# A transformer mixer on one core: ScalarE issues a store and a load, the first router layer and `x` of layer 1 in other banks, `product` 0 and the norm's `scale` moved

## The chip, the cores and the metric

One core of a Trainium2 chip runs the kernel. The metric is the device time of one execution in microseconds; below half a per cent or so nothing is claimed.

## The reference

Input `x` is 8 x 1024 tokens of 256 numbers. The output is the input plus two branches of its layer norm:

```python
xn = _layernorm(x)
x = x + attn(xn) + ffn(xn)
# attn: 16 heads of 16; heads 0-3 causal over all 1024 keys, heads 4-15 causal over the last 64;
#       softmax, times V, times w_out, plus biases
# ffn, with Q = xn @ W_Q.T, K = xn @ W_K.T and a second pair Q @ W_inv.T, K @ W_inv.T:
xV = einsum('btd,kdr->btkr', Q_side, V)            # 8 experts of 64
cum_yW = cumsum(einsum('btd,kdr->btkr', K_side, W), axis=1)
h = gelu(Q_side @ router_w1.T + router_b1)         # router, exact gelu
weights = softmax(h @ router_w2.T + router_b2 + expert_bias)
out = einsum('btkr,kdr->btd', xV * cum_yW * weights[..., None], U) + weights @ b
out = out / n_valid
# ffn = (fwd + alpha * inv) @ W_O.T
```

## The kernel before, in words

The weights of all layers are folded once at the start: `W_O` into `U`, `W_Q` into the router and `V`. Every float32 product that needs full precision is made of three of fp32r parts (high x high, high x low, low x high; helper `mms`, L684). Then 16 chunks of 512 tokens pass (two per sequence). A chunk with an even number is the first half of a sequence and has few blocks of global attention (6 tiles of 128 keys x 256 queries), one with an odd number has 14.

The order of work is written out by hand. `Plan.add` lists stages (`x`, `c`, `weigh`, `product`, `gscore`, ...), `weave` mixes a main list with a side list, and each of the five engine programs walks the one list and issues its own part of each stage. So the place of a stage in the list sets its place in the in-order queue of every engine, SyncE with its DMA issues among them. `uses` names the PSUM bank (0 to 7) that a stage takes; the n-th user waits until the one before it is read out.

One chunk `ch` passes these phases, while the next one is prepared:

- **experts and peaks.** For each of 8 expert layers j: `x` (6 matmuls, bank 2, copied by ScalarE to `prod[j % 3]`, L1039), `weigh` (GpSimd multiplies it by the spread router weights in `wide[j % 3]`, L1517), `c` (6 matmuls, bank 3), `product` (VectorE multiplies bank 3 into `prod`, L1323; ScalarE makes the high part PH, L1049; GpSimd the low part PL, L1522), `mix` (TensorE sums onto the output in banks 0 and 1, L795). `c` of layer j+1 can't begin before `product` j has read bank 3. Between them stand the peaks: TensorE computes all scores once (L817 local, L831 global, banks 4 to 7) over masks that ScalarE lays down (L1055), and VectorE takes the largest of each row (L1240, L1247).
- **local attention**, with the next chunk's `turn`, `parts` (queries and keys in three bf16 parts; VectorE L1211 reads the bank), and `hidden` (first router layer, 4 x 6 matmuls, banks 2, 3, 4, 3).
- **global attention**: `gscore` (L890), exponentials (L1075), `gav` (L908), and in their midst `logits`, `gates`, `gate_parts` (router softmax on VectorE, L1279 to L1316), `values`, and the norm of chunk `ch + 2` in nine steps (`NORM`; the last, `scale`, is L1174).
- **handover**: `weigh` 0, `x` 1, `weigh` 1, `cturn` and `chigh` of the context's second half (L1351, L1081), `x` 2, `weigh` 2, `crest` (L1356), then the next chunk's first group, which was `product` 0.

The router weights travel through DRAM: `gate_parts` stores `weights_t` in four DMAs of 8 rows to `weights_d` (L1648) and the bf16 rows to `rows_d` (L1654); `wide` loads each row spread over 64 partitions (L1678), two DMAs per layer; `weight_rows` loads `WT` (L1663) for `open`, the bias matmul (L761). All DMAs are issued by SyncE. Ahead of the store stand the `stacks` of the next chunk (eight DMAs, `area<-parts_d`, L1605), behind it `Vs` (L1618) and the global stacks (L1607).

## Time and profile before

| | |
|---|---|
| median of 3 runs | 1487.54 us (1483.8 to 1489.47) |
| the profiled execution | 1489.6 us, span 1487.9 us |
| granted clock, mean | 0.983 |
| busy: TensorE, VectorE, ScalarE, GpSimd | 92%, 68%, 52%, 39% |
| DMA: bytes, share of the 16 engines by SyncE's queue | 150.59 MB, 39.1% |

The profile is of one execution. TensorE is the busiest engine; the share of the others is an average over phases of different kinds, and has to be read phase by phase. A wait in the views is the idle time of an engine just before an instruction, with what ended it.

### The profile page before, as it was taken

The numbers are of one execution on the slowest core, as the hardware profiler recorded it, in microseconds if no ns is written. First come the engines' busy times: TensorE is split into PE (matmuls) and PEld (weight loads), VectorE is DVE, ScalarE is ACT, GpSimd is POOL, SyncE is SP. The second block draws the span as 40 slices with busy tenths as digits, with TensorE's granted clock in tenths as the row PEclk, the third lists the DMA queues.
The fourth block names the chain that finished last, engine by engine and source line by source line (L and its number), as shares of the span: only waits on it lengthen the run. The fifth ranks groups of instructions, "written<-read, shape, count | busy, mean of one in ns | idle before, by whom it ended". The sixth has DMA issues, their size and how long they took to land.

```text
span 1487.9 us, 35980 instructions
## 1 busy us (share of the span) xinstructions
PE 1368.7 (92%) x14481; PEld 1034.5 (70%) x14481; DVE 1004.9 (68%) x2082; ACT 775.5 (52%) x1368; POOL 580.1 (39%) x663
## 2 busy tenths in 40 slices
PE   5978999999999989998999999999999989999986
PEld 4567685777848677586867768577775868667673
DVE  6667777567755867567775667567885577756661
ACT  2434537464564635645375554646356453755544
POOL 1024343443424344253434524244452434345350
PEclk9999999999999999999999999999999999999997
DMA  8430625326162541616344171623517153441610
GB/s 186 106 94 25 164 70 130 116 67 160 44 158 67 124 123 48 168 33 152 95 117 113 40 187 39 155 90 100 148 38 175 35 147 100 112 117 41 175 37 15
DMA packets 166614, 152.88 MB, mean 103 GB/s; under 512 B 37809, under 2 KB 149808, under 8 KB 166448
## 3 DMA queue, kind: packets, MB, share of 16 engines
q1 hardware_dynamic: 166448, 150.59, 39.1%
q8 instruction: 114, 1.87, 0.5%
q14 instruction: 52, 0.43, 0.1%
HBM read 108.57 MB, written 35.65 MB: 97 GB/s over the span
## 4 chain that ended last, share of the span: by engine, by line
PE 64%; DVE 13%; ACT 7%; issue 7%; DMA 5%; POOL 1%; SPq 1%; ACTq 0%; POOLq 0%; DVEq 0%
PE PS L684 32%; PE PS L795 10%; PE PS L831 4%; DMA weights_d<-weights_t 3%; ACT HE L1075 3%; PE PS L890 3%; PE PS L919 3%; PE PS L817 2%; DVE prod L1211 2%; PE PS L973 2%; PE PS L908 2%; DMA rest<-weights_d 2%; ACT HE L1067 2%; DVE area L1214 1%; PE PS L876 1%
## 5 line engine op out<-in xcount | busy, mean ns | idle before, releaser
L684 PE MATMUL PS<-XH,WH 128*128 128x512 f32 x512 | 219.8, 429 | 29.1 <-DVE prod L1211 14.5
L1522 POOL TENSOR_TENSOR PL<-prod,PH 128x512 fp32r<-128x512 f32 x128 | 164.9, 1289 | 207.9 <-ACT PH L1049 207.9
L1049 ACT ACTIVATE PH<-prod 128x512 fp32r<-128x512 f32 x128 | 80.8, 632 | 272.9 <-DVE prod L1323 257.0
L1517 POOL TENSOR_TENSOR prod<-prod,rest 128x512 f32<-128x512 f32 x96 | 123.1, 1284 | 244.2 <-DMA rest<-weights_d 167.8
L1247 DVE TENSOR_REDUCE block_peak<-PS 128x4 f32<-128x512 f32 x288 | 179.8, 684 | 49.0 <-PE PS L831 48.9
L684 PE MATMUL PS<-XH,WL 128*128 128x512 f32 x512 | 203.7, 398 | 0.0
L684 PE MATMUL PS<-XL,WH 128*128 128x512 f32 x512 | 203.5, 398 | 0.0
L1075 ACT ACTIVATE HE<-PS 128x512 f32<-128x512 f32 (+1 forms) x320 | 159.9, 552 | 34.4 <-PE PS L890 31.6
L1500 POOL TENSOR_SCALAR_AFFINE_SELECT HE<-HE 128x256 f32<-128x256 f32 x128 | 51.5, 408 | 305.5 <-ACT HE L1075 302.0
L1323 DVE TENSOR_TENSOR prod<-PS,prod 128x512 f32<-128x512 f32 x128 | 87.8, 686 | 100.2 <-PE PS L684 79.0
L684 PEld LDWEIGHTS PS<-XH,WH 128*128 128x128 f32 x512 | 96.9, 189 | 70.4 <-DVE prod L1211 21.1
L1039 ACT ACTIVATE prod<-PS 128x512 f32<-128x512 f32 x128 | 75.7, 591 | 114.5 <-PE PS L684 104.2
L795 PE MATMUL PS<-UH,PH 128*128 128x256 f32 x512 | 133.1, 293 | 0.0
L684 PE MATMUL PS<-CH,WH 128*128 128x512 f32 x256 | 109.6, 428 | 24.7 <-DVE prod L1323 24.7
L1240 DVE TENSOR_REDUCE peak<-PS 128x4 f32<-128x512 f32 x192 | 119.0, 682 | 19.1 <-PE PS L817 19.1
L795 PE MATMUL PS<-UL,PH 128*128 128x256 f32 x512 | 127.5, 282 | 0.0
L1339 DVE STREAM_TRANSPOSE craw<-PS 128x512 f32<-128x512 f32 x64 | 45.5, 712 | 102.3 <-PE PS L908 96.4
L684 PEld LDWEIGHTS PS<-XH,WL 128*128 128x128 f32 x512 | 96.8, 189 | 22.5
L890 PE MATMUL PS<-area 99*128 99x256 bf16 (+1 forms) x640 | 101.4, 267 | 10.5 <-ACT HE L1075 7.3
L684 PEld LDWEIGHTS PS<-XL,WH 128*128 128x128 f32 x512 | 97.8, 191 | 14.2
L1067 ACT ACTIVATE HE<-PS 128x512 f32<-128x512 f32 x192 | 105.2, 594 | 2.4 <-PE PS L851 2.4
L684 PE MATMUL PS<-CH,WL 128*128 128x512 f32 x256 | 103.8, 406 | 0.0
(190 smaller groups left out, 3047.9 us busy)
## 6 DMA issues: line engine op xcount, KB each, us to landing
parts_d<-area SPq DMA_DIRECT2D x32, 768.0 KB, 5.0
area<-parts_d SPq DMA_DIRECT2D x128, 192.0 KB, 7.9
rest<-weights_d SPq DMA_DIRECT2D x192, 128.0 KB, 3.0
area<-parts_d SPq DMA_DIRECT2D x32, 576.0 KB, 7.9
tok<-in_L_attn_x_dram SPq DMA_DIRECT2D x16, 512.0 KB, 6.3
xt<-in_L_attn_x_dram SPq DMA_DIRECT2D x16, 512.0 KB, 4.2
wide<-weights_d SPq DMA_DIRECT2D x64, 128.0 KB, 3.1
out_dram<-xt SPq DMA_DIRECT2D x16, 512.0 KB, 3.8
```

What stands on the lines that cost most here:

```text
L684: ins = e.matmul(ps, a, b, start=first and k == 0, stop=last and k == n - 1, skip_group_check=True)
L795: ins = e.matmul(out_half(t), (PH, PL)[part][:, h, t * P:(t + 1) * P], u[:, j, :], start=False, stop=False, skip_group_check=True)
L890: ins = e.matmul(psum(i, lo=HALF * a + lo, hi=HALF * (a + 1)), KG[0:KSTK, g, j * P:(j + 1) * P], QS[0:KSTK, g, half * HALF + lo:(half + 1) ...
L1039: e.activation(prod[:, j % 3, :], psum(2), ACT.Copy).then_inc(bank_read[2])
L1049: e.activation(PH[:, h, :], prod[:, j % 3, :], ACT.Copy).then_inc(phi)
L1067: e.activation(HE[:, k, :], psum(i), ACT.Exp, scale=SCALE).then_inc(bank_read[i])
L1075: e.activation(two(HE[:, k, :], lo), two(psum(i), lo), ACT.Exp, scale=SCALE).then_inc(bank_read[i])
L1240: e.tensor_reduce(peak[:, t, 4 * grp:4 * (grp + 1)], psum(i).rearrange("p (a k) -> p a k", a=4), AX_X, ALU.max).then_inc(bank_read[i])
L1247: e.tensor_reduce(block_peak[ch % NC][:, t, :, j], psum(i).rearrange("p (a k) -> p a k", a=4), AX_X, ALU.max).then_inc(bank_read[i])
L1323: e.tensor_tensor(prod[:, r, :], psum(3), prod[:, r, :], ALU.mult).then_inc(bank_read[3])
L1517: e.tensor_tensor(prod[:, j % 3, :], prod[:, j % 3, :], wide[j % WIDE], ALU.mult).then_inc(weighed)
L1522: e.tensor_tensor(PL[:, j % 2, :], prod[:, j % 3, :], PH[:, j % 2, :].bitcast(F32), ALU.subtract).then_inc(plo)
```

## The change

- `weights_d` becomes a copy of `weights_t` (128 x 256) and is stored in one DMA, for all chunks. `wide` reads each row in two halves of 256.
- In odd chunks (`by_scalar`) ScalarE issues this store (after `values` 0) and the first `wide` load (after the last but two of the global groups). In even chunks SyncE still does.
- For all chunks SyncE's bf16 store (`weight_parts`) comes behind the first `wide` loads instead of ahead of them.
- `hidden` uses banks 4, 2, 3, 4. `x` of layer 1 uses bank 7 from chunk 1 on.
- `product` 0 is added behind `chigh` and ahead of `x` 2.
- `scale` of the norm moves from the global phase of one chunk to behind the first group of peaks in the next, from chunk 2 on.

```diff
@@ -114,6 +114,10 @@
+    def x_bank(ch, j):
+        return 7 if ch and j == 1 else 2
@@ -191,14 +195,14 @@
     def add_hidden(ch, j):
-        add_on("hidden", ch, j, uses=[f"bank{(2, 3, 4, 3)[j]}", exp_use()])
+        add_on("hidden", ch, j, uses=[f"bank{(4, 2, 3, 4)[j]}", exp_use()])
...
     def add_x(ch, j, part):
-        add("x", ch, j, part, uses=["bank2"] if part == 0 else [])
+        add("x", ch, j, part, uses=[f"bank{x_bank(ch, j)}"] if part == 0 else [])
@@ -267,7 +271,8 @@
             order.append([(add_c, ch, j, part) for part in range(2)] if j else [])
-            order[-1].append((add_product, ch, j))
+            if j or not ch:
+                order[-1].append((add_product, ch, j))
             if j:
@@ -296,9 +301,14 @@
         add("gate_parts", ch)
-        for j in range(WIDE):
+        for j in range(1 if by_scalar(ch) else 0, WIDE):
             add_wide(ch, j)
+        add("weight_parts", ch)
         add("weight_rows", ch)
+    def by_scalar(ch):
+        return ch % NC == 1
@@ -309,8 +319,9 @@
         at_ = len(order) // 3
-        for n in range(len(NORM)):
-            order[at_ + n * (len(order) - at_) // len(NORM)].append((add, "norm", ch, n))
+        steps = len(NORM) - (1 if ch > 1 else 0)
+        for n in range(steps):
+            order[at_ + n * (len(order) - at_) // steps].append((add, "norm", ch, n))
@@ -397,6 +408,8 @@
         run(experts[0] + peaks[0])
+        if ch and nxt:
+            add("norm", ch + 1, len(NORM) - 1)
         weave(experts[1:split], peaks[1:])
@@ -433,6 +446,9 @@
             side += [[(add_values, ch + 1, 0)], [(add_values, ch + 1, 1)]]
+            if by_scalar(ch + 1):
+                side[-2].append((add, "weights_store", ch + 1))
+                order[-3].append((add_wide, ch + 1, 0))
             side[0].append((add, "crest", ch, 0))
@@ -447,6 +463,7 @@
         if nxt:
+            add_product(ch + 1, 0)
             run([(add_x, ch + 1, 2, part) for part in range(2)])
@@ -537,7 +554,7 @@
         peak_d = [nc.dram_tensor(f"peak_d_{n}", (3 * k, C), BF16, kind="Internal").ap() for n, k in (("local", NL), ("global", NG))]
-        weights_d = nc.dram_tensor("weights_d", (2 * KE, C), F32, kind="Internal").ap()
+        weights_d = nc.dram_tensor("weights_d", (P, HALF), F32, kind="Internal").ap()
         rows_d = nc.dram_tensor("rows_d", (3, 2 * KE, C), BF16, kind="Internal").ap()
@@ -673,6 +690,29 @@
+        def store_weights(e, q, ch):
+            q.wait_ge(weights_turned, ch + 1)
+            for i in range(WIDE):
+                q.wait_ge(wide_in[i], 16 * 2 * (use(f"wide{i}", "wide", ch, i) - 1))
+            e.dma_start(weights_d, weights_t[:, :]).then_inc(weights_out, 16)
+        def load_weights(e, q, ch, j):
+            q.wait_ge(weights_out, 16 * (ch + 1))
+            if j >= WIDE:
+                q.wait_ge(weighed, nth("weigh", ch, j - WIDE))
+            elif j == 2:
+                q.wait_ge(weighed, nth("weigh", ch - 1, 5))
+            else:
+                q.wait_ge(part3, nth("parts", ch, 0, DB - 1))
+                q.wait_ge(clo, DB * (ch + 1))
+                if ch == 0:
+                    q.wait_ge(bias_in, 16 * 15)
+            by_half = weights_d[2 * 32 * (j // KB):2 * 32 * (j // KB + 1), :].rearrange("(h e) t -> e h t", h=2)
+            for k in range(2):
+                n = 2 * (j % KB) + k
+                e.dma_start(wide[j % WIDE][R * k:R * (k + 1), :].rearrange("p (h t) -> p h t", h=2), by_half[n:n + 1].to_broadcast([R, 2, HALF])).then_inc(wide_in[j % WIDE], 16)
@@ -738,7 +778,7 @@
                     ch, = key
-                    q.wait_ge(bank_read[3], use("bank3", "hidden", ch, 3))
+                    q.wait_ge(*out_of_bank("hidden", ch, 3))
                     take(7, *stage)
@@ -763,10 +803,11 @@
                     ch, j, part = key
+                    i = x_bank(ch, j)
                     if part == 0:
-                        take(2, *stage)
+                        take(i, *stage)
                     n = 3 * part
-                    ins = mms(psum(2), weight_pairs(COL_X + j * P, XH, XL)[n:n + 3], first=part == 0, last=part == 1)
+                    ins = mms(psum(i), weight_pairs(COL_X + j * P, XH, XL)[n:n + 3], first=part == 0, last=part == 1)
                     if part == 1:
@@ -1024,6 +1065,14 @@
+                elif kind == "weights_store":
+                    store_weights(e, q, *key)
+                elif kind == "wide":
+                    ch, j = key
+                    if j == 0 and by_scalar(ch):
+                        load_weights(e, q, ch, j)
                 elif kind == "x":
@@ -1036,7 +1085,8 @@
                                 q.wait_ge(part3, nth("parts", ch, 0, j // 2))
-                        e.activation(prod[:, j % 3, :], psum(2), ACT.Copy).then_inc(bank_read[2])
+                        i = x_bank(ch, j)
+                        e.activation(prod[:, j % 3, :], psum(i), ACT.Copy).then_inc(bank_read[i])
@@ -1306,7 +1356,7 @@
                     q.wait_step()
-                    q.wait_ge(weights_out, 16 * 4 * ch)
+                    q.wait_ge(weights_out, 16 * ch)
                     q.wait_ge(rows_cast, ch)
@@ -1512,7 +1562,8 @@
                     ch, j = key
-                    q.wait_ge(bank_read[2], use("bank2", "x", ch, j, 0))
+                    i = x_bank(ch, j)
+                    q.wait_ge(bank_read[i], use(f"bank{i}", "x", ch, j, 0))
                     q.wait_ge(wide_in[j % WIDE], 16 * 2 * use(f"wide{j % WIDE}", "wide", ch, j))
@@ -1639,13 +1690,11 @@
                     ch, = key
-                    q.wait_ge(weights_turned, ch + 1)
-                    for i in range(WIDE):
-                        q.wait_ge(wide_in[i], 16 * 2 * (use(f"wide{i}", "wide", ch, i) - 1))
-                    for w in range(2):
-                        for h in range(2):
-                            row = 32 * (2 * w + h)
-                            e.dma_start(weights_d[KE * w:KE * (w + 1), h * HALF:(h + 1) * HALF], weights_t[row:row + KE, :]).then_inc(weights_out, 16)
+                    if not by_scalar(ch):
+                        store_weights(e, q, ch)
+                elif kind == "weight_parts":
+                    ch, = key
                     q.wait_ge(rows_cast, ch + 1)
@@ -1664,18 +1713,8 @@
                     ch, j = key
-                    q.wait_ge(weights_out, 16 * 4 * (ch + 1))
-                    if j >= WIDE:
-                        q.wait_ge(weighed, nth("weigh", ch, j - WIDE))
-                    elif j == 2:
-                        q.wait_ge(weighed, nth("weigh", ch - 1, 5))
-                    else:
-                        q.wait_ge(part3, nth("parts", ch, 0, DB - 1))
-                        q.wait_ge(clo, DB * (ch + 1))
-                        if ch == 0:
-                            q.wait_ge(bias_in, 16 * 15)
-                    for k in range(2):
-                        e.dma_start(wide[j % WIDE][R * k:R * (k + 1), :], weights_d[2 * j + k:2 * j + k + 1, :].to_broadcast([R, C])).then_inc(wide_in[j % WIDE], 16)
+                    if j or not by_scalar(ch):
+                        load_weights(e, q, ch, j)
```

How the rows move at the handover from chunk 2 to chunk 3, which stands for all eight into an odd chunk. Line numbers differ between the two kernels.

ScalarE, from the last exponentials to `product` 0, before:

```order
L1075 ACTIVATE HE<-PS 128x512 [waits he5_read,gscores_ps]
L1075 ACTIVATE HE<-PS 128x512 [waits he0_read,gscores_ps]
L1008 ACTIVATE Va<-PS 128x32x16 [waits values_ps]
L1075 ACTIVATE HE<-PS 128x2x128 [waits he1_read,gscores_ps]
L1075 ACTIVATE HE<-PS 128x2x128 [waits he2_read,gscores_ps]
L1039 ACTIVATE prod<-PS 128x512 [waits plo,x_ps]
L1081 ACTIVATE PH<-craw 128x512 [waits split1_read,ctx_turned]
L1039 ACTIVATE prod<-PS 128x512 [waits part3,x_ps]
L1049 ACTIVATE PH<-prod 128x512 [waits split0_read,bank3_read_out]
```

and with the change:

```order
L1049 ACTIVATE Va<-PS 128x32x16 [waits values_ps,vs_in]
L697 DMA weights_d<-weights_t 128x256 [waits wide1_in,wide2_in,wide0_in,weights_turned]
L1125 ACTIVATE HE<-PS 128x512 [waits he5_read,gscores_ps]
L1125 ACTIVATE HE<-PS 128x512 [waits he0_read,gscores_ps]
L1049 ACTIVATE Va<-PS 128x32x16 [waits values_ps]
L1125 ACTIVATE HE<-PS 128x2x128 [waits he1_read,gscores_ps]
L1125 ACTIVATE HE<-PS 128x2x128 [waits he2_read,gscores_ps]
L714 DMA rest<-weights_d 64x2x256 [waits clo,part3,weights_out]
L714 DMA rest<-weights_d 64x2x256
L1089 ACTIVATE prod<-PS 128x512 [waits plo,x_ps]
L1131 ACTIVATE PH<-craw 128x512 [waits split1_read,ctx_turned]
L1099 ACTIVATE PH<-prod 128x512 [waits split0_read,bank3_read_out]
```

The two kinds of DMA are new on this engine, the load waits for the store's landing (`weights_out`), and PH (L1099, before L1049) stands ahead of the copy of `x` 2.

SyncE, from the weights' store to the rows' loads, before:

```order
L1648 DMA weights_d<-weights_t 8x256 [waits wide1_in,wide2_in,wide0_in,weights_turned]
L1648 DMA weights_d<-weights_t 8x256 x3
L1654 DMA rows_d<-weights_b 3x8x256 [waits rows_in,rows_cast]
L1654 DMA rows_d<-weights_b 3x8x256 x3
L1678 DMA rest<-weights_d 64x512 [waits clo,weights_out]
L1678 DMA rest<-weights_d 64x512 x3
L1678 DMA wide<-weights_d 64x512 [waits weighed]
L1678 DMA wide<-weights_d 64x512
L1663 DMA WT<-rows_d 48x1x512 [waits opened,rows_out]
L1663 DMA WT<-rows_d 32x1x512
```

and with the change:

```order
L714 DMA rest<-weights_d 64x2x256 [waits clo,weights_out]
L714 DMA rest<-weights_d 64x2x256
L714 DMA wide<-weights_d 64x2x256 [waits weighed]
L714 DMA wide<-weights_d 64x2x256
L1703 DMA rows_d<-weights_b 3x8x256 [waits rows_in,rows_cast]
L1703 DMA rows_d<-weights_b 3x8x256 x3
L1712 DMA WT<-rows_d 48x1x512 [waits opened,rows_out]
L1712 DMA WT<-rows_d 32x1x512
```

The store and one pair of loads are gone, and the four issues to `rows_d` stand behind the loads.

VectorE, from the context's last transposition to the second peaks, before:

```order
L1343 TENSOR_TENSOR ctok<-craw,cinv 128x16x16 [waits dve_step]
L1174 TENSOR_SCALAR tok<-tok,mv,var 128x256 [waits dve_step]
L1174 TENSOR_SCALAR tok<-tok,mv,var 128x256 x3
L1351 STREAM_TRANSPOSE craw<-ctok 128x512
L1356 TENSOR_TENSOR PL<-craw,PH 128x512 [waits ctx_hi]
L1323 TENSOR_TENSOR prod<-PS,prod 128x512 [waits c_ps,weighed]
L1240 TENSOR_REDUCE peak<-PS 128x4 [waits lpeaks_ps] x4
L1323 TENSOR_TENSOR prod<-PS,prod 128x512 [waits c_ps,weighed]
L1367 TENSOR_TENSOR xt<-PS,xt 128x512 [waits out_ps,residual_in]
L1367 TENSOR_TENSOR xt<-PS,xt 128x512 [waits split1_read]
```

and with the change:

```order
L1393 TENSOR_TENSOR ctok<-craw,cinv 128x16x16 [waits dve_step]
L1219 TENSOR_SCALAR var<-var 128x4 [waits dve_step]
L1221 TENSOR_TENSOR var<-var 128x4 [waits dve_step]
L1401 STREAM_TRANSPOSE craw<-ctok 128x512 [waits dve_step]
L1373 TENSOR_TENSOR prod<-PS,prod 128x512 [waits c_ps,weighed]
L1406 TENSOR_TENSOR PL<-craw,PH 128x512 [waits ctx_hi]
L1290 TENSOR_REDUCE peak<-PS 128x4 [waits lpeaks_ps] x4
L1224 TENSOR_SCALAR tok<-tok,mv,var 128x256 x4
L1373 TENSOR_TENSOR prod<-PS,prod 128x512 [waits c_ps,weighed]
L1417 TENSOR_TENSOR xt<-PS,xt 128x512 [waits out_ps,residual_in]
L1417 TENSOR_TENSOR xt<-PS,xt 128x512 [waits split1_read]
```

`scale` (L1174, now L1224) has gone from ahead of `cturn` to behind four peak reductions, `product` (L1323, now L1373) ahead of `crest` (L1356, now L1406).

## Rows read from the trace of the kernel before

**Rows 1.** The page, busy time of each engine.

```profile
PE 1368.7 (92%) x14481; PEld 1034.5 (70%) x14481; DVE 1004.9 (68%) x2082; ACT 775.5 (52%) x1368; POOL 580.1 (39%) x663
```

**Rows 2.** TensorE's waits, whole span: for whom, us in total, times, longest.

```profile
PE PS L684 <- DVE prod L1323: 24.7, 11, 3.7
PE PS L684 <- DVE prod L1211: 14.5, 15, 1.0
...
PE PS L684 <- ACT prod L1039: 10.3, 15, 0.7
```

**Rows 3.** The same view, from 160 to 1487 us.

```profile
PE PS L684 <- DVE prod L1323: 17.5, 8, 3.7
```

**Rows 4.** Three of eight stretches at odd handovers: busy times, PEclk, DMA, GB/s.

```profile
339.00:361.00 22.00, 19.28 (x176) 14.91 (x174) 16.45 (x46) 10.88 (x20) 7.95 (x9) 0.92 0.65 159
513.00:535.00 22.00, 17.64 (x164) 13.40 (x164) 15.20 (x45) 8.30 (x16) 7.18 (x9) 0.84 0.63 150
...
1036.00:1058.00 22.00, 19.24 (x203) 13.89 (x202) 17.98 (x57) 11.26 (x22) 8.32 (x11) 1.00 0.76 170
```

**Rows 5.** The chain that ended last, 340 to 352.2: start, us, what.

```profile
340.08 6.16 DMA weights_d<-weights_t
...
346.82 3.06 DMA rest<-weights_d
350.01 1.27 POOL prod L1517
351.31 0.70 DVE prod L1323
352.06 0.51 PE PS L684
```

**Rows 6.** Timeline of TensorE: first and third group of local peaks.

```profile
348.94 1.08 PE L817 MATMUL PS<-area 96*64 96x128 bf16 x32
...
361.09 1.08 PE L817 MATMUL PS<-area 96*64 96x128 bf16 x32
```

**Rows 7.** Stretches; the last three columns are PEclk, DMA share, GB/s.

```profile
340.00:345.00 5.00, 5.00 (x53) 3.76 (x52) 4.32 (x23) 1.64 (x4) 1.55 (x4) 1.00 1.02 197
...
366.00:371.00 5.00, 5.00 (x42) 4.27 (x40) 4.56 (x9) 2.44 (x4) 3.06 (x3) 1.00 0.22 59
```

**Rows 8.** Timeline of SyncE's DMA issues: start, us of all issues, line, what.

```profile
339.07 1.30 SPq L1648 DMA_DIRECT2D weights_d<-weights_t  x4
340.47 3.03 SPq L1654 DMA_DIRECT2D rows_d<-weights_b  x4
346.25 2.44 SPq L1678 DMA_DIRECT2D rest<-weights_d  x4
...
350.07 1.93 SPq L1663 DMA_DIRECT2D WT<-rows_d  x3
...
353.56 5.22 SPq L1607 DMA_DIRECT2D area<-parts_d  x8
...
365.68 3.41 SPq L1635 DMA_DIRECT2D peak_d_local<-peak_t_local  x4
370.35 0.28 SPq L1638 DMA_DIRECT2D area<-peak_d_local  x1
```

**Rows 9.** Timeline of ScalarE, 338 to 361.

```profile
341.86 0.66 ACT L1075 ACTIVATE HE<-PS 128x256 f32<-128x256 f32 x2 [0.18 <-PE PS L890]
345.82 0.60 ACT L1039 ACTIVATE prod<-PS 128x512 f32<-128x512 f32 x1 [3.30 <-PE PS L684]
...
358.02 2.40 ACT L1055 ACTIVATE PS<-peak_mask_l 128x512 f32<-128x512 bf16 x4 [0.63 <-DVE peak L1240]
```

**Rows 10.** Timeline of VectorE, 346 to 356.

```profile
346.12 1.38 DVE L1174 TENSOR_SCALAR tok<-tok,mv,var 128x256 f32<-128x256 f32 x4
...
351.92 2.48 DVE L1240 TENSOR_REDUCE peak<-PS 128x4 f32<-128x512 f32 x4
...
355.49 0.69 DVE L1367 TENSOR_TENSOR xt<-PS,xt 128x512 f32<-128x512 f32 x1 [0.50 <-PE PS L919]
```

## The prediction

> **What bounds the kernel now.** I read the page first. TensorE is busy for 92% of the span [rows 1], so anything that delays it delays the end, and anything hidden under it is free. The view of TensorE's waits then tells which delays the change can touch. Three kinds stand there [rows 2]: a multiplication waits for VectorE's `product` (L1323) 24.7 us in 11 cases, the first router layer for VectorE's query part (L1211) 14.5 us in 15, `x` for ScalarE's copy out of bank 2 (L1039) 10.3 us in 15. After 160 us the first kind is 17.5 us in 8 cases, the longest 3.7 [rows 3]: once per handover into an odd chunk (0 to 1, 2 to 3, ... 14 to 15). The other 7.2 us lie before 160 us, in the start-up, and I leave them alone. The 15 of the other two kinds are one per handover, about 0.97 and 0.69 us each.
>
> The stretches around the 8 odd handovers show what such a wait costs beyond itself [rows 4]: the granted clock of TensorE, 1.00 elsewhere, is 0.92 over 22 us in five of them, 0.84 in the one with the 3.7 us wait, 1.00 in two. That is 5 x 1.76 + 3.5 = 12.3 us of lost matmul time: after the idle stretch TensorE runs for a while at 1.2 instead of 2.4 GHz.
>
> The chain of waits at the handover 2 to 3 says who is late [rows 5]: the weights' store to DRAM lands 6.16 us after its last issue, the spread load takes 3.06, the weighing on GpSimd 1.27, `product` on VectorE 0.70, and only then `c` of layer 1 starts at 352.06. TensorE was ready at 350.02, when its peak matmuls (L817, 348.94 + 1.08) were done [rows 6]. Why does a 32 KB store take 6.16 us? The 16 DMA engines are busy all the time from 340 to 345 (1.02), with the stacks of the next chunk, which SyncE issued just before on the same queue; from 366 to 371 the share is 0.22 [rows 7], and there the small peak store is waited out 1.26 us after its issues (365.68 + 3.41 to 370.35) [rows 8]. So the store stands in line behind the stacks.
>
> **The change part by part**, at that handover.
>
> 1. Banks of the first layer. Hidden 1 no longer takes the bank that L1211 has yet to read; it takes bank 2, free earlier, and hidden 2, which takes bank 3, comes 1.4 us later. Bank 4 was used in this place before. The wait of 0.97 goes: 15 x 0.97 = **-14.5**. `x` of layer 1 in bank 7 takes away the wait of `x` of layer 2 for the copy: 15 x 0.69 = **-10.3**. ScalarE and GpSimd do the same work, and nothing else in rows 2 waits there.
>
> 2. Store by ScalarE. The store is one DMA of 128 x 256 (128 KB) for four of 8 KB. The weights turn 1 us earlier (term 1), at 338.1; in ScalarE's order the issue stands behind a copy, and I take 338.4, against SyncE's last of four, which ended at 339.07 + 1.30 = 340.4 [rows 8]. No row shows a DMA issued by ScalarE. Its landing is bounded below by the 1.26 us of the peak store plus 128 KB at the 197 GB/s of [rows 7] (0.65) and an issue, some 2.5 us, above by the 6.16 us of the store in line, a little more for its size. I take 3.6, nearer the short end, because its queue holds nothing else: it lands at 342.0. By the Trainium skill (DMA: Bandwidth & Descriptors, Queues, rings and completion order) SP and ACT each own one row of rings and every DMA engine goes round between the rows packet by packet, which would let it overtake; the same page (Issuing engines are not separate DMA queues) says that issuing from several engines only saves the sequencer's time. No run here shows either; the second is a rival below.
>
> 3. First spread load by ScalarE. It waits for the landing behind the last exponentials, which end at 342.5 before [rows 9], 341.8 now. Two issues of 0.6, landing 3.06 after the second begins (pieces of 1 KB for 2 KB: 0 to 0.6 more), 1.27 and 0.70 [rows 5]: 342.0 + 0.6 + 3.1 + 2.0 = 347.7. TensorE is ready at 350.0 - 1.7 = 348.3. The wait goes with 0.6 us to spare: **-17.5**, and the clock with it: **-12.3**.
>
> 4. `scale` of the norm (1.38 us on VectorE) leaves the path before `cturn`, and moves behind the first four peak reductions; `product` 0 now goes ahead of the rest of the context. With `product` done at 347.7 VectorE goes on: rest of the context 348.4, four reductions of 0.62 to 350.9, `scale` 352.3, `product` 1 353.0, two additions of 0.69 354.4, four reductions 356.9 [rows 10]. Each reduction lets ScalarE write a mask of 0.60 [rows 9]: the last is ready at 357.5. TensorE's third group of peaks came 361.09 - 352.06 = 9.0 us after `c` [rows 6], of which 1.7 were the slow clock; it would begin at 348.3 + 7.3 = 355.6 and end a microsecond later, and now ends at 357.8. Cost 1.2, taken as 1.5: 8 x 1.5 = **+12**. At the even handovers TensorE comes only 1.7 us earlier, and I take nothing.
>
> 5. ScalarE's issues. The store's takes 0.3 to 0.65 us (SyncE's of 8 rows and of 128) out of a stretch in which TensorE waits for exponentials: 8 x 0.6 = **+4.8**. What else queues behind the two issues of the load is the copy of `x` 1, which before had waited 3.30 us for TensorE [rows 9]: no cost, if the store has landed. For the load and SyncE's neighbouring loads colliding I add 8 x 0.5 = **+4**.
>
> 6. SyncE's order. Now loads 1 and 2 (four issues, 2.44 us), the bf16 rows' store (3.03), its landing (1.26 as the peak store), then the rows' loads (1.93), `Vs` (1.56 up to 353.56) and the global stacks (5.22) [rows 8]. Before, the last issue ended at 358.8; now 342.0 + 15.4 = 357.4, 1.4 us earlier, while TensorE is 4 us earlier. The last stack is in some 3.1 us after its issue begins, at 360.0. Its first reader, two pieces of 1.5 us behind the third group of peaks, comes at 361. No cost, but a microsecond of cover; if it is gone, the global peaks are late next. At the even handovers, where the same order puts the rows behind three loads, TensorE's phase is longer and I take nothing.
>
> Sum: -14.5 - 10.3 - 17.5 - 12.3 + 12 + 4.8 + 4 = **-33.8**. The profiled execution took 1489.6 us (span 1487.9), 2 us above the median 1487.5 of the runs shown; the same difference from the median gives **1454**.
>
> **The rivals.** (A, forecast) as above, 0.60.
>
> (B) The store overtakes, but the gain runs into VectorE and SyncE. VectorE is busy for 16.45 of 22 us there [rows 4]; if the third group waits 3 us and not 1.5, and the rows or global stacks come a microsecond late, 8 x 2.5 = 20 us go back: 1474, or 1470 if one holds in part. For it: the margins of 1 us in terms 3 and 6. Against it: these waits would have to lie wrong by a microsecond in all eight, and a wait that only moves along the path is counted once. 0.20, at 1471.
>
> (C) The store doesn't overtake: it waits for the stacks and lands at 346.0. Then ScalarE stands still from 341.8, `product` ends at 351.7 and `c` starts 0.35 us earlier than before, but with a wait of 3.4 us in place of 2.0. The handover at 513 had such a wait, and its clock was 0.84 for 0.92: 1.7 us more. 8 x (1.7 - 0.35) = +10.8 against 15 waits for the copies of which the 7 even handovers keep 1.66 each, -11.6: about no change, 1487. This is what the skill's second sentence would give. 0.12.
>
> (D, slower) ScalarE becomes the gate. Its queue is in order, and in odd chunks the first mask is in bank 7, which waits for the copy of `x` 1, which waits behind the load, which waits for the store. If the store lands at 347.6, 1.6 us later than in C, each odd handover is 2.95 us longer: +23.6 - 11.6 = +12, 1499. It passes the half per cent from a landing at 347.1, some 8.5 us after the issue. For it: four times the bytes, twice the pieces in the loads, two queues at once on full DMA engines. Against it: 6.16 us is what the whole line took. 0.08.
>
> **How the numbers follow.** A measurement of this kernel can tell about 0.5% (7.4 us) from no change. A and B are faster, C is within, D slower; a few cases of C fall on either side: faster 0.81, same 0.11, slower 0.08. The range goes down to 1442, where terms 4 to 6 cost half of what I put, and up to 1482, past B and to the edge of C.
>
> **What would show it.** Right: no wait for L1373 (the new line of `product`) after 160 us, none for the query part, none for the copy of `x`; a granted clock of 1.00 at the handovers; the store landing within 4 us of its issue while the stacks still move; new small waits of TensorE at the peaks (L817's successor) of 1 to 1.5 us. Wrong: `weights_d` still in the chain with 6 us, ScalarE idle until it lands, TensorE waiting for a mask or for `product` over 3 us at odd handovers; or the waits gone and the time the same, which would mean that the peaks or the global stacks took their place.

## The result, and the profile after

The changed kernel takes 1492.36 us (median of 18 runs, 1487.78 to 1497.88), the kernel before on the same chip 1486.33 (18 runs). The ratio is 1.004, 95% interval 1.0029 to 1.0051: 6.0 us slower (4.3 to 7.6), which is the near edge of what a measurement can tell from no change. Forecast were 1454 and a range of 1442 to 1482; the result lies outside it. The profiled execution took 1492.45 us, its span is 1490.7; the spans of the two profiled executions (1490.7 and 1487.9) are 2.8 us apart, less than half of what the medians are. Of the executions of the later runs, two passed at a low clock throughout (2119.69 us at 0.559, 1638.86 us at 0.75), and the medians given leave them out.

The page of the changed kernel, busy times and DMA queues:

```profile
PE 1371.8 (92%) x14481; PEld 1042.8 (70%) x14481; DVE 1006.3 (68%) x2082; ACT 773.5 (52%) x1368; POOL 582.6 (39%) x663
...
q1 hardware_dynamic: 180656, 149.01, 39.8%
q10 hardware_dynamic: 3456, 3.15, 0.8%
```

Queue q10 is new: it is ScalarE's. TensorE is 3.1 us longer busy than in [rows 1] with the same instructions, and its mean granted clock is 0.975 for 0.983, so more of the time passed at 1.2 GHz. How much of the 3.1 us is the clock's isn't settled: busy time does not follow the clock alone (one of the runs below has 0.975 with 1366.5 us).

TensorE's waits in the whole span (for whom, us in total, times, longest), which answer to [rows 2]:

```profile
PE PS L724 <- DVE prod L1373: 27.1, 11, 3.6
PE PS L844 <- ACT prod L1089: 18.3, 8, 3.2
...
PE PS L801 <- DMA WT<-rows_d: 3.8, 1, 3.8
```

The waits of 14.5 and 10.3 us are gone, all 30 of them, as forecast. But `product` (L1373) is waited for 2.4 us more, and there are two new waits: in 8 handovers 18.3 us for ScalarE's copy out of bank 7 (L1089, ahead of the first mask), and once, at 97.6 us in chunk 0, 3.8 us for the bf16 rows (0.2 before). The sum of these waits was 24.7 + 14.5 + 10.3 + 0.2 = 49.7 us and is 27.1 + 18.3 + 3.8 = 49.2; that with the 3.1 us of longer busy time makes +2.6, and the spans differ by 2.8. The waits have moved, not gone.

The chain of waits at the handover 2 to 3 (start, us, what), which answers to [rows 5]:

```profile
339.01 8.65 DMA weights_d<-weights_t
347.68 0.63 ACTq L714
348.33 4.86 DMA rest<-weights_d
353.33 1.27 POOL prod L1568
354.63 0.70 DVE prod L1373
355.37 2.93 PE PS L724 x6
```

`c` of layer 1 starts at 355.37, 3.3 us later than before. The store is issued a microsecond earlier than the last of four in [rows 8], and lands 8.65 us after that, at 347.66, instead of at 346.24. The load takes 4.86 for 3.06.

The landing is better counted from the stacks. SyncE's issue of the eight local stacks, in the kernel before:

```profile
330.12 5.38 SPq L1605 DMA_DIRECT2D area<-parts_d  x8
```

and in the changed kernel, with the load that waits for the store:

```profile
331.26 5.39 SPq L1656 DMA_DIRECT2D area<-parts_d  x8
347.67 1.26 SPq L714 DMA_DIRECT2D rest<-weights_d  x2
```

So 1.1 of the 3.3 us were there already when the stacks were issued. From the start of that issue to the weights' landing it is 16.1 us before and 16.4 with the change, though the last issue of the store comes 10.0 us after that start before and 7.75 us now. The weights came 2.2 us earlier against the stacks and landed no earlier.

ScalarE stands still meanwhile. Its timeline, with the idle time before an instruction in brackets, against [rows 9]:

```profile
339.01 0.33 ACTq L697 DMA_DIRECT2D weights_d<-weights_t  x1
...
341.78 0.66 ACT L1125 ACTIVATE HE<-PS 128x256 f32<-128x256 f32 x2 [0.18 <-PE PS L931]
347.68 1.53 ACTq L714 DMA_DIRECT2D rest<-weights_d  x2
349.31 0.60 ACT L1089 ACTIVATE prod<-PS 128x512 f32<-128x512 f32 x1 [6.88 <-issue]
```

The last exponentials end at 342.44; then nothing until the store has landed. The copy of `x` 1, which before waited for TensorE, comes at 349.31, and TensorE, which needs its bank for the first mask, waits for it.

Why the store needs 8.65 us shows in the DMA queues (packets, MB, share). First the stretch 341 to 343, two microseconds after the store's issue, then 345 to 347:

```profile
q1 hardware_dynamic: 450, 0.45, 111.3%
```

```profile
q1 hardware_dynamic: 175, 0.16, 38.7%
q10 hardware_dynamic: 144, 0.13, 24.9%
```

From 339 to 345 no packet of q10 is moved; the first packet of q10 is moved in 345 to 345.5, six microseconds after its issue, when the stacks are nearly through. The store is 144 packets. By the Trainium skill (DMA: Bandwidth & Descriptors, Queues, rings and completion order) every DMA engine goes round between the rings packet by packet; with that, packets of q10 should stand beside those of q1 from 339 or 340 on, and the trace does not agree. The other sentence of the same page in the Trainium skill that the prediction drew on (Issuing engines are not separate DMA queues), that issuing from several engines saves only the sequencer's time, fits what is seen.

The granted clock at the same stretches as [rows 4] (last columns PEclk, DMA share, GB/s):

```profile
339.00:361.00 22.00, 16.63 (x126) 12.78 (x126) 13.32 (x40) 7.23 (x15) 6.74 (x8) 0.77 0.66 142
513.00:535.00 22.00, 17.75 (x172) 13.04 (x171) 13.65 (x45) 8.07 (x16) 6.77 (x8) 0.92 0.72 146
...
1036.00:1058.00 22.00, 15.96 (x139) 12.06 (x138) 13.21 (x44) 8.33 (x16) 6.76 (x8) 0.92 0.71 146
```

Over the seven such stretches from 339 on the clock is three times 0.77 or 0.78 and four times 0.92; before it was four times 0.92, once 0.84 and twice 1.00. With two waits of about 3 us in each, where there was one of about 2, more of the stretch passes at 1.2 GHz.

### The profile page after: what moved, and what is told of

Read it like the earlier page. It is cut to its first block, busy times and chain, and to the rows that moved or that the text cites. A ratio compares the mean times of both kernels' runs of the same rounds, so it can differ in the third digit from the quotient of the medians.

```text
span 1490.7 us, 35948 instructions
## 1 busy us (share of the span) xinstructions
PE 1371.8 (92%) x14481; PEld 1042.8 (70%) x14481; DVE 1006.3 (68%) x2082; ACT 773.5 (52%) x1368; POOL 582.6 (39%) x663
## 4 chain that ended last, share of the span: by engine, by line
PE 68%; DMA 8%; DVE 7%; ACT 7%; issue 5%; POOL 3%; SPq 0%; ACTq 0%; POOLq 0%; DVEq 0%
PE PS L724 35%; PE PS L836 10%; DMA weights_d<-weights_t 5%; PE PS L872 4%; ACT HE L1125 3%; PE PS L931 3%; PE PS L960 3%; DMA rest<-weights_d 3%; PE PS L917 3%; PE PS L858 2%; ACT HE L1117 2%; PE PS L1014 2%; PE PS L949 2%; PE PS L892 2%; DVE prod L1373 1%
## 5 line engine op out<-in xcount | busy, mean ns | idle before, releaser
L1573 POOL TENSOR_TENSOR PL<-prod,PH 128x512 fp32r<-128x512 f32 x128 | 168.6, 1318 | 202.4 <-ACT PH L1099 202.3
L1099 ACT ACTIVATE PH<-prod 128x512 fp32r<-128x512 f32 x128 | 80.8, 631 | 278.2 <-DVE prod L1373 274.4
L724 PE MATMUL PS<-XH,WH 128*128 128x512 f32 x512 | 216.7, 423 | 4.5 <-DVE rest L1242 1.8
L1373 DVE TENSOR_TENSOR prod<-PS,prod 128x512 f32<-128x512 f32 x128 | 87.6, 685 | 130.7 <-PE PS L724 69.0
L1089 ACT ACTIVATE prod<-PS 128x512 f32<-128x512 f32 x128 | 75.6, 590 | 134.2 <-PE PS L724 89.0
L724 PE MATMUL PS<-CH,WH 128*128 128x512 f32 x256 | 112.1, 438 | 27.1 <-DVE prod L1373 27.1
L1290 DVE TENSOR_REDUCE peak<-PS 128x4 f32<-128x512 f32 x192 | 118.9, 682 | 15.3 <-PE PS L858 14.5
```

Of the source, the lines that this page charges most:

```text
L724: ins = e.matmul(ps, a, b, start=first and k == 0, stop=last and k == n - 1, skip_group_check=True)
L1089: e.activation(prod[:, j % 3, :], psum(i), ACT.Copy).then_inc(bank_read[i])
L1099: e.activation(PH[:, h, :], prod[:, j % 3, :], ACT.Copy).then_inc(phi)
L1290: e.tensor_reduce(peak[:, t, 4 * grp:4 * (grp + 1)], psum(i).rearrange("p (a k) -> p a k", a=4), AX_X, ALU.max).then_inc(bank_read[i])
L1373: e.tensor_tensor(prod[:, r, :], psum(3), prod[:, r, :], ALU.mult).then_inc(bank_read[3])
L1573: e.tensor_tensor(PL[:, j % 2, :], prod[:, j % 3, :], PH[:, j % 2, :].bitcast(F32), ALU.subtract).then_inc(plo)
```

## The experiments

The theory after reading the trace: the weights' landing is set by the stacks of the next chunk that are already on their way, from whatever engine the store is issued; so terms 2 and 3 fail, the banks' gain of term 1 turns into a longer wait for `product`, and ScalarE's part adds a wait of its own. The main rivals: ScalarE as the issuer is what makes the store late (its position or its queue); or the new layout (one store of 128 KB, pieces of 1 KB) does.

In all of them the landings are read at the seven odd handovers from 339 us on, from the (last) issue of the store. Counted from the start of the issue of the eight stacks instead, to the issue that waits for the landing, the means of the seven are 16.2 us before, 15.9 with the change, and 15.9 to 16.4 in the five runs that leave the stacks alone. There the issuer, the layout and the time of the store's issue make no difference beyond half a microsecond. It is 13.1 to 14.1 us in the four runs with five of the eight DMAs ahead of the store, 11.3 in the split of the changed kernel with four, and 9.5 with nearly empty stacks.

### SyncE issues everything

```diff
     def by_scalar(ch):
-        return ch % NC == 1
+        return False
```

> The changed kernel, but SyncE issues the weights' store and all spread loads in every chunk. Theory 1 (ScalarE's queue does not overtake the stacks, and its copy of x 1, queued behind the load, holds up the first mask): the 18.3 us in 8 waits of the masks for the copy vanish, the wait for product stays since the 128 KB store still lands some 8 us after its issue; 1483 to 1488. Theory 2 (the moved product, scale and bf16 rows are what costs): nothing changes, 1491 to 1494.

Measured: 1488.7 us, ratio 1.0023 (1.0007 to 1.0038), just above the 1483 to 1488 that was expected. The wait for the mask is gone, that for `product` is longer (the view from 160 to 1480 us):

```profile
PE PS L724 <- DVE prod L1373: 38.1, 8, 5.5
```

It was 22.5 us, and the masks' 18.3; the two together were 40.8 us and are 38.1. The interval overlaps that of the changed kernel (1.0029 to 1.0051), so the times alone don't tell the two apart.

The store lands after 8.3 us in the mean of seven (6.8 to 9.2), against 8.1 (7.1 to 9.0) with ScalarE. The issuer makes no difference of half a microsecond. The load takes 3.5 us and not 4.9, now that loads 1 and 2 follow it on the same queue instead of starting beside it.

### ScalarE issues the store alone, SyncE the loads

```diff
-        for j in range(1 if by_scalar(ch) else 0, WIDE):
+        for j in range(WIDE):
...
-                order[-3].append((add_wide, ch + 1, 0))
```

> ScalarE issues the store in odd chunks, SyncE all loads. Theory 1: as with SyncE issuing both, within 3 us of it, because the first packet of the store still waits for the stacks' last; no wait of a mask for the copy. If ScalarE's queue overtook the stacks when SyncE's loads are not beside it, the store would land within 4 us and the time would be near 1460.

Measured: 1484.41 us, 0.9992 (0.9975 to 1.0009). Product wait 36.2 us in 8, no wait for a mask; landing 8.1 us in the mean. Against the changed kernel (1.0029 to 1.0051) this is about 7 us better by the ratios, and the intervals are apart: what costs is the blocking load in ScalarE's order, not the store. Against the kernel with SyncE alone it is 4 us better, where within 3 was expected, but those intervals touch.

### GpSimd issues the store

```diff
-            e.dma_start(weights_d, weights_t[:, :]).then_inc(weights_out, 16)
+            e.dma_start(weights_d, weights_t[:, :]).then_inc(landed(ch)[0], 16)
```

The step stands in GpSimd's part of the program for odd chunks, and `landed` names a semaphore of its own for it; SyncE issues the loads.

> As the run in which ScalarE issued only the store, but GpSimd issues it, on its own queue with descriptors made in another way. If the DMA engines themselves serve what came first, whatever its queue, the store lands 8 us after its issue again and the time is 1484 to 1490. If what held ScalarE's store was that its descriptors are made behind SyncE's, it moves among the stacks and lands within 4 us, product's wait falls from 36 us to under 10, and the time is 1452 to 1465.

Measured: 1486.99 us, 1.0014 (0.9999 to 1.003); landing 7.9 us (6.9 to 8.7), product wait 37.7 us in 8. The store at this handover was issued at 336.75. The queues from 340 to 343, 3 us later:

```profile
q1 hardware_dynamic: 599, 0.57, 110.8%
q0 software_dynamic: 8, 0.03, 4.7%
```

The software queue gets 8 packets through beside 599, all in the last microsecond; 39 more are moved from 343 to 344, when the stacks are nearly through. So neither a second hardware queue nor the software one passes the stacks, and the landing within 4 us that the expectation put beside this fails.

### The banks alone, on the kernel before

```diff
-        add_on("hidden", ch, j, uses=[f"bank{(2, 3, 4, 3)[j]}", exp_use()])
+        add_on("hidden", ch, j, uses=[f"bank{(4, 2, 3, 4)[j]}", exp_use()])
...
-        add("x", ch, j, part, uses=["bank2"] if part == 0 else [])
+        add("x", ch, j, part, uses=[f"bank{x_bank(ch, j)}"] if part == 0 else [])
```

> The kernel before with the two changes of banks alone (hidden in 4, 2, 3, 4; x 1 in bank 7). Theory 1: the 24.8 us of waits for the query part and the copy vanish; the store still lands when the stacks are through, so at the 8 odd handovers most of the 1.7 us gained turn into a longer wait for product: 17.5 grows to 25 to 31 us and the time is 1470 to 1478. If the store's landing moved with its issue, product's wait would stay near 23 and the time would be near 1465.

Measured: 1481.72 us, 0.998 (0.9963 to 0.9997), some 3 us (0.4 to 5.5) of the 24.8 us of waits that it removes. The expectation, 1470 to 1478 us with 25 to 31 us of waits for `product`, was too good:

```profile
PE PS L688 <- DVE prod L1329: 36.8, 8, 5.5
```

Product was waited for 17.5 us [rows 3]; now 36.8, which takes back 19.3 of the 24.8. The store's last issue comes 1.2 us earlier after the start of the stacks (8.8 for 10.0 us at the handover 2 to 3), and the landing after the issue is 7.5 us in the mean for 6.2 before: the earlier issue is waited out in full.

### The old layout, with SyncE issuing all

Against the first experiment the store is again four DMAs of 8 rows, and the loads read pieces of 2 KB:

```diff
-        weights_d = nc.dram_tensor("weights_d", (P, HALF), F32, kind="Internal").ap()
+        weights_d = nc.dram_tensor("weights_d", (2 * KE, C), F32, kind="Internal").ap()
...
-            e.dma_start(weights_d, weights_t[:, :]).then_inc(weights_out, 16)
+            for w in range(2):
+                for h in range(2):
+                    row = 32 * (2 * w + h)
+                    e.dma_start(weights_d[KE * w:KE * (w + 1), h * HALF:(h + 1) * HALF], weights_t[row:row + KE, :]).then_inc(weights_out, 16)
```

> The changed kernel with SyncE issuing store and loads and with the layout of before (four stores of 8 rows, rows of 2 KB in the spread loads); what is left of the change are the banks, product 0 and scale in their new places, and the bf16 rows behind the loads. Theory 1: the layout costs 0.5 to 1 us at each odd handover (the loads took 3.4 to 3.6 us from 1 KB pieces against 3.0), so 1482 to 1485, between the banks alone (1481.7) and all by SyncE (1488.7). Theory 2 (the moves cost): it stays at 1488 and the layout is worth nothing.

Measured: 1484.12 us, 0.9998 (0.998 to 1.0015); product wait 35.7 us in 8; landing 7.5 us, loads 2.9 to 3.1 (once 4.1). By these runs the layout costs about half a microsecond per load and some 3 to 4 us in all, though the interval overlaps that of the first experiment. It is not what makes the store late.

### Few stacks

From chunk 2 on the local stacks copy one of 12 heads (part of the local attention's inputs is left out); all else is as changed:

```diff
+                                n = NL if ch < 2 else 1
+                                e.dma_start(KL[rows, :n, WINDOW:] if w else QS[rows, NG:NG + n, :], src[:, NG:NG + n, :]).then_inc(local_in, 16)
```

> The changed kernel with the local stacks of chunks 2 to 15 copying one head of twelve (the other heads keep old data, so the local attention of these chunks is computed on wrong numbers). It asks whether the stacks are what the store waits for. Theory 1: the store lands 2.5 to 3.5 us after its issue, the waits of masks and of product vanish, the clock stays at 1.00 at odd handovers, time 1450 to 1462. If the landing is slow in itself (its size, its target, ScalarE's queue): still 6 us and more, and 1485 to 1492.

Measured: 1451.84 us, 0.976 (0.9731 to 0.979). The queue and the store's issue between 343 and 345 (KB each, us to landing), then TensorE's waits from 160 to 1480:

```profile
q10 hardware_dynamic: 144, 0.13, 18.6%
issues: line engine op xcount, KB each, median us to landing
weights_d<-weights_t ACTq DMA_DIRECT2D x1, 128.0 KB, 1.7
```

```profile
PE PS L724 <- DVE prod L1373: 3.9, 3, 3.2
PE PS L858 <- ACT PS L1105: 3.3, 17, 0.4
...
PE PS L844 <- ACT prod L1089: 1.9, 1, 1.9
```

Without the stacks the same store by the same engine lands in 1.7 us, both waits all but go, the granted clock is 1.00 at the seven later odd handovers (TensorE busy 1362.8 us for 1371.8), and the time is 40 us under the changed kernel. That the stacks hold up the store is shown from the other side. The 40 us are more than the price of that, since the even chunks' stacks are gone as well. The run also prices term 4: with `product` in time, the masks of the peaks (L1105) are waited for 3.3 us in 17 cases (0.4 in 2 before), not 12. ScalarE's load, beside SyncE's, still takes 4.2 to 4.6 us; that part of its time is not due to the stacks.

### Part of the stacks behind the store

The local stacks need not all stand ahead of the store: their first reader is the first group of local peaks, at 348.94 before [rows 6]. In odd chunks SyncE issues the keys' stacks, then the weights' store, then the queries' stacks, then the loads:

```diff
+        if ch % NC == 1:
+            add("late_stacks", ch, "local")
...
+                        if reach == "local" and w == (1 if late else 0) and ch % NC == 1:
+                            continue
```

> The changed kernel with SyncE issuing all, and in odd chunks the stacks of the queries (half of the bytes) behind the weights' store instead of ahead of it. Theory 1: the stacks of the keys are through when the store is issued, it lands in 2 to 3 us, product's wait shrinks from 38 us to 0 to 10; new small waits of the peaks for the stacks of the queries; 1452 to 1466. If the peaks wait for the queries by more than a microsecond each time: 1466 to 1480.

Measured: **1464.02 us, 0.9857** (0.9836 to 0.9879), 1.4% better than the kernel before and 1.8% better than the changed one. TensorE's wait from 160 to 1480, and the chain at this handover:

```profile
PE PS L726 <- DVE prod L1375: 15.8, 8, 2.1
```

```profile
339.55 3.72 DMA weights_d<-weights_t
343.95 6.20 DMA rest<-weights_d
```

The store lands in 3.7 us, not the 2 to 3 expected, and `product` is waited for 15.8 us, not up to 10: the load stands behind the queries' stacks and takes 6.2.

The same on the kernel with the banks alone, the rest as before the change:

> The kernel before with the banks alone, and the same split of the stacks; product 0 and scale in their old places. Theory 1: 1455 to 1470, up to 5 us above the same split in the changed kernel if the new places of product 0 and scale are worth something once the store is early, and below it if the later scale costs the 1.5 us per odd handover that the prediction gave it.

Measured: 1468.27 us, 0.9894 (0.9875 to 0.9913); product 19.8 us in 8, and 7.0 us in 8 for stacks that come late. So the gain needs nothing of ScalarE's part. With the layout, the norm and SyncE's order of the change it is some 5 us better; the intervals just touch.

### Where to split

Half the queries' stacks stay ahead of the store, the other three DMAs stand right behind it:

```diff
+                        for n, (rows, i) in enumerate(STACK):
+                            if reach == "local" and ch % NC == 1 and late != (w == 0 and n > 0):
+                                continue
```

> After with SyncE issuing all; in odd chunks only the key stacks and the first query DMA stand ahead of the weights' store, the other three query DMAs right behind it and ahead of the loads. Theory (the landing of the store is set by what its own queue has not yet moved): the store lands 2.5 to 4 us after its issue, the loads behind 1.5 MB less than in the first split, product waits under 10 us in 8 handovers (15.8 in the first split), time 1455 to 1463. Rival (any stacks in flight delay store and loads alike, wherever they stand): product waits 13 to 18 us again, 1464 within 2 us.

Measured: 1466.9 us (1465.06 to 1469.71), 0.986 (0.9842 to 0.9879). The theory's numbers failed: product wait 20.8 us in 8, not under 10, and the store lands in 4.7 to 7.3 us, not 2.5 to 4. The rival's 13 to 18 us and 1464 within 2 were nearer. The chain:

```profile
334.86 6.35 DMA weights_d<-weights_t
341.22 0.61 SPq L716
341.88 3.67 DMA rest<-weights_d
```

From the store's issue to the load's landing it is 10.7 us here, 10.6 in the split before, and 12.8 with everything ahead of the store (8.68, a 0.6 us issue, 3.5). How the stacks are divided around the store makes no difference to the load's landing, as the rival had it: in both runs all of them are ahead of the load. What either split saves is 2.1 to 2.2 us. I read it as the time in which the store was on its way and waited out with nothing left on the queue; it is filled with late stacks now. No run separates that from other readings.

The three DMAs behind the first load:

> The same, with the three late query DMAs behind the first load instead of ahead of it. Theory: load 0 lands about 3 us after its issue, as with few stacks, and product waits under 5 us; time 1452 to 1460 unless the global or local peaks now wait for the query stacks. Rival (the late stacks are the next gate): a wait for DMA of the query stacks of over 1 us per odd handover, time 1460 to 1468.

Measured: 1485.51 us (1478.03 to 1487.41), 0.9973 (0.996 to 0.9987). The rival named the right gate, but its 1460 to 1468 us was far too low: the new waits take back nearly all of the gain. From 160 to 1480:

```profile
PE PS L860 <- DMA area<-parts_d: 32.5, 8, 5.6
```

Nothing waits for `product` any more; the first peaks wait for the queries' stacks, 4.1 us in the mean of 8. Weights and stacks are needed within a few microseconds of each other, and they share the same DMA engines.

The first of these two with the old layout, and that one again with `product` 0 and `scale` in their old places:

> The first of these with the stores of 8 rows and pieces of 2 KB in the loads, as before the change. Theory (the layout costs 0.5 us at each odd handover while product is late): 3 to 4 us under it. If product is no longer late there: no difference within 1.5 us, since nothing waits for the half microsecond.

> The one before with product of tile 0 ahead of the context and scale ahead of the turn in their old places. Tells what term 4 is worth. By the forecast's working (+12 for the move) this would be 8 to 12 us faster; by the reading of the run with few stacks (a wait for masks of 0.4 us per handover) it is within 3 us or up to 5 us slower, since the path to product is 1.4 us longer again.

Measured: 1464.69 us, 0.9847 (0.9828 to 0.9867), and 1467.56, 0.9855 (0.9834 to 0.9877). The layout's 3 to 4 us don't show here: the medians are 2.2 us apart (1466.9 and 1464.69), well within the intervals. The places of `scale` and `product` make no difference that can be told, where the forecast had put +12 on them; putting them back should then have saved 8 to 12 us, and by the ratios it cost 1 us, with intervals of some 3 us to either side.

## Why the prediction was wrong

**What bounds the kernel** was read rightly: the store in line behind the stacks, and the clock after an idle stretch. Without most of the stacks the changed kernel takes 1451.84 us, near the forecast 1454. That nearness is luck in part: the forecast adds 54.6 us of gains and 20.8 of costs, while between the two profiles TensorE's idle time fell by 31.3 us and its busy time by 5.9, and the even chunks lost stacks too.

**Term 2 failed**, the landing of the store behind the stacks: "I take 3.6, nearer the short end, because its queue holds nothing else". It measured 8.65 at that handover and 8.1 in the mean. The low bound (2.5) was sound for idle engines: 1.7 in the run with few stacks. The choice between the ends was the error, and the evidence was at hand: a DMA share of 1.02 [rows 7] says that the engines themselves had no room. A queue of its own put the store ahead of nothing, and no row showed two queues at once. The upper end, "6.16 us of the store in line, a little more for its size", was also too low: the landing is tied to the stacks, and so it grows by what the issue is earlier, 2.2 us here (8.65 for 6.16).

**Term 3 failed with it**: -17.5 and -12.3 became +5.0 from 160 us on (17.5 to 22.5 us of `product`), 18.3 us for the mask, and a mean clock of 0.975 for 0.983. Of its own errors: the load took 4.9 and not 3.1 with SyncE's loads beside it. And the way in which it priced the clock, lost share times 22 us, is too dear: counted so, the loss would have grown from 12.3 to some 24 us, while TensorE's busy time grew by 3.1. The stretches contain the waits themselves.

**Term 1** was right as waits (24.8 us gone) and wrong as time. Alone it brings 3 us: of a cover that goes, term 6 says that "the global peaks are late next", but term 1 was priced as if terms 2 and 3 were certain. A gain ahead of a fixed arrival only lengthens the wait for it: 17.5 to 36.8.

**Term 4** was too large: 3.3 us of mask waits in place of 12 where `product` was in time, and no difference in the last pair of runs.

**Term 5**: the store's issue on ScalarE costs nothing that can be measured. The load on ScalarE costs about 7 us against the run that differs in this alone, and mostly for another reason than the forecast's collisions: it blocks the copy.

**Term 6** held after the start-up, but missed chunk 0. There the bf16 store now stands behind three loads, and TensorE waits 3.8 us for the rows (0.2 before). The stacks of chunk 1 are issued at 157.1 us for 155.9 before, and at 153.0 with the banks alone.

**Rivals.** The result is D's mechanism at 8.65 us landing: ScalarE blocked, the first mask waiting for the copy. Its place and its cause were right, its chance of 0.08 far too low, and its +12 too high by six. Part of that is the mean landing, 8.1 and not 8.65: 8 x 0.5 = 4 us, an estimate. C described the same landing, 1.6 us earlier. Both rest on a store that doesn't overtake, and together they had 0.20 against 0.80 for one that does, with no row for either; that split was the real misjudgement.

**Open**: why the other queues' packets are not served while the stacks move. The traces show only when packets are moved, not where they stand in between. Whether part of the 2.2 us that a split saves is the time in which the queue stood empty is argued and not shown. A spread load straight from the on-chip tile, without the trip through DRAM, wasn't tried, and neither were stacks issued earlier.

## What to carry to other kernels

Before a DMA is moved to another engine's queue to overtake, read the DMA share: here it was 1.0 for microseconds ahead, and none of three issuers won anything; putting part of the bulk behind the small store did. That brought 1.4%, with no new engine, as long as the bulk moved back stayed ahead of the second transfer; behind it, the bulk itself came late and the gain was gone. An issue that waits for a landing held up all that stood behind it in ScalarE's order, so look for an engine which has nothing else that others wait for. When a landing doesn't move with its issue, count it from the work that it waits for; and price a wait that you remove only up to the next fixed arrival.

## What the hardware showed

- A store of 128 KB (144 packets) landed in 1.7 us with nearly empty stacks and in 6.8 to 9.2 us behind the stacks, with SyncE, ScalarE or GpSimd as the issuer. ScalarE's first packet was moved 6 us after its issue.
- An issue on ScalarE takes 0.33 us for this store (SyncE's 0.34). The two issues of the load take it 1.53 us together in the changed kernel and 1.24 with few stacks, where SyncE's two take 1.26.
- Of two loads at once from two queues, the one on ScalarE's takes 4.9 us in the mean, and 4.2 to 4.6 with nearly empty stacks. With all loads on SyncE's queue, one behind the other, the first takes 3.5.
